# Expert rows scattered into a slot-sorted DRAM table and turned in 32x32 blocks on VectorE, instead of gathered per tile and turned on TensorE

## The chip, the cores and the metric

The kernel runs on one core of a Trainium2 chip. The metric is the device time of one execution in microseconds (us). All five engines (TensorE, VectorE, ScalarE, GpSimd, SyncE) run their own instruction streams, which are written out by hand and meet at semaphores.

## The reference

A gated cross-attention block over 4 batches of 512 tokens with 512 features, then a mixture-of-experts FFN with 16 experts, of which each token takes 4, and a shared FFN.

```python
x = x + jnp.tanh(g_xattn[0]) * _L0_xattn_ref(_layernorm(x), mask, ctx_2048, ctx_2048, wq, wk, wv, wo)
x = x + jnp.tanh(g_ffn[0]) * _L0_ffn_ref(_layernorm(x), Wg, W1, W2, W3, W1s, W2s, W3s)

def _moe_forward(hidden_states, Wg, W1, W2, W3, W1s, W2s, W3s):
    x = hidden_states.reshape(-1, D)                                  # T = 2048 tokens, D = 512
    shared = jax.nn.silu(x @ W1s.T) * (x @ W3s.T) @ W2s.T             # 704 hidden
    probs = jax.nn.softmax((x @ Wg.T).astype(jnp.float32), axis=-1)   # 16 experts
    topk_w, sel = jax.lax.top_k(probs, TOP_K)                         # 4 of them
    combine = jnp.zeros((T, E), x.dtype).at[jnp.arange(T)[:, None], sel].add(topk_w)
    h = jax.nn.silu(jnp.einsum('td,efd->etf', x, W1)) * jnp.einsum('td,efd->etf', x, W3)   # 352 hidden
    routed = jnp.einsum('etf,edf->td', h * combine.T[:, :, None], W2)
    return shared + routed
```

## The kernel before

Every float32 product is made of three products of a high and a low part (`tripled`, the matmuls of L86). A high part is a rounded copy, a low part the difference of the raw value and the high part.

The program has four stages, one after the other, with a barrier of all engines between two of them.

*Attention* (0 to 436 us) goes batch by batch. SyncE loads the batch's x twice (`x_t` for the sums and `r_t` for the residual, 1 MB each) and the context, and stores x2 (the residual stream, 1 MB) and xn2 (the normalised input of the FFN, 1 MB) to DRAM. The router's probabilities and ranks of the experts are made here.

*Routing* (436 to 552 us): TensorE makes the shared FFN of batches 0 and 1 in the class `Shared`: per batch 6 blocks of hidden columns, then 4 row tiles. Beside it VectorE does the routing, in pieces that `work` assigns to places between the shared FFN's own operations (place 0 to 5 stand behind the blocks of the first batch, 6 to 9 behind its row tiles, and so on). Each of the 2048 x 4 choices gets a slot: slots are sorted by expert, and each expert's slots are filled up to a multiple of 128, a tile. With the drawn inputs there are 72 tiles (the expert of most has 4 or 5). `counts` makes the slot numbers from two small matmuls of the masks, `choose` picks the slot and the weight of each choice, `number` splits slot numbers, and `one_hot` writes 128 masks, with which TensorE makes the list `slot_tokens` (which token stands in each slot) in 64 matmuls at the end of the stage. GpSimd subtracts the first expert's weights (`split_expert`: in pieces of 512 columns here), loads the second expert's high part, and gathers tile 0.

*Experts* (552 to 1051 us) walk over the tiles, four in a loop body, on every engine. GpSimd gathers a tile's 128 rows from `xn_dram` by the slot list into one of four buffers `xg`. For tile t TensorE turns the 128x512 rows in four 128x128 transposes into `c_ps_x`, ScalarE copies the high part to `xT_hi`, VectorE subtracts the low part `xT_lo`. TensorE meanwhile makes the output product of tile t-2 (`c_ps_y`), the transposes of the hidden rows of tile t-1 (`c_ps_h`), and then the 24 products of tile t (`c_ps_u`). ScalarE makes `gate`, VectorE `hf`. GpSimd also loads each further expert's weights, high and raw, in three buffers, and subtracts them (3840 + 512 columns). SyncE stores only 16 tiles of zeros, behind the last tile.

*Combining* (1051 to 1168 us): the shared FFN of batches 2 and 3, and 64 indirect gathers (L1596) of each token's four expert rows.

The padding slots of a tile hold token 0 in the list, and their results are never read.

## Time and profile before

| what | value |
|---|---|
| median of 3 runs (lowest, highest) | 1171.72 us (1171.42, 1180.43) |
| the profiled execution | 1170.14 us, span 1168.5 us |
| mean granted TensorE clock | 0.977 |
| TensorE busy | 1106.2 us (95%) |
| VectorE busy | 490.0 us (42%) |
| ScalarE busy | 279.6 us (24%) |
| GpSimd busy | 477.5 us (41%) |
| moved by DMA | 199.70 MB |

The profile is of one execution. The span runs from its first to its last instruction; the execution's own time is 1.6 us longer. In the rows below a line number is the kernel's line, `PE` is TensorE, `DVE` VectorE, `ACT` ScalarE, `POOL` GpSimd and `SPq` SyncE's DMA issues. What stands in brackets is the engine's idle time ahead of the row and what ended it. Matmul starts are exact, their ends modelled, so the pace of TensorE is read from one start to the next.

### The profile page before, as it was taken

The numbers are of one execution on the slowest core, as the hardware profiler recorded it, in microseconds if no ns is written. First come the engines' busy times: TensorE is split into PE (matmuls) and PEld (weight loads), VectorE is DVE, ScalarE is ACT, GpSimd is POOL, SyncE is SP. The second block draws the span as 40 slices with busy tenths as digits, with TensorE's granted clock in tenths as the row PEclk, the third lists the DMA queues.
The fourth block names the chain that finished last, engine by engine and source line by source line (L and its number), as shares of the span: only waits on it lengthen the run. The fifth ranks groups of instructions, "written<-read, shape, count | busy, mean of one in ns | idle before, by whom it ended". The sixth has DMA issues, their size and how long they took to land. (4 is left out here: it accounts for less than half of the span.)

```text
span 1168.5 us, 18611 instructions
## 1 busy us (share of the span) xinstructions
PE 1106.2 (95%) x5666; PEld 940.0 (80%) x5667; DVE 490.0 (42%) x994; ACT 279.6 (24%) x575; POOL 477.5 (41%) x521
## 2 busy tenths in 40 slices
PE   3999999999999959998989999999999999988997
PEld 3888878878878827686879999999999999977775
DVE  2243463445336255996222222222222222225847
ACT  1231131122113002111223333333333333321210
POOL 4720201201100235101665565556656665617763
PEclk9999999999999968899999999999999999998999
DMA  9411320312220528133864666666666666627785
GB/s 348 193 73 73 122 94 1 141 74 72 108 72 0 225 85 297 36 111 96 325 226 162 216 229 229 238 220 222 236 220 229 229 220 229 215 69 237 226 278 162
DMA packets 54209, 199.70 MB, mean 171 GB/s; under 512 B 7009, under 2 KB 7009, under 8 KB 45985
## 3 DMA queue, kind: packets, MB, share of 16 engines
q0 software_dynamic: 21184, 122.44, 30.1%
q1 hardware_dynamic: 22624, 57.98, 13.9%
q10 hardware_dynamic: 10368, 18.88, 4.3%
q8 instruction: 18, 0.29, 0.1%
q14 instruction: 15, 0.11, 0.0%
HBM read 161.51 MB, written 37.75 MB: 171 GB/s over the span
## 5 line engine op out<-in xcount | busy, mean ns | idle before, releaser
L86 PE MATMUL c_ps_u<-expert_hi,xT_hi 128*128 x576 | 192.7, 335 | 2.0 <-DVE xT_lo L1445 1.9
L86 PE MATMUL c_ps_u<-expert_hi,xT_lo 128*128 x576 | 186.0, 323 | 0.0
L86 PE MATMUL c_ps_u<-expert_lo,xT_hi 128*128 x576 | 185.6, 322 | 0.0
L986 POOL TENSOR_TENSOR expert_lo<-expert_raw,expert_hi (+3 forms) x39 | 158.2, 4079 | 19.9 <-issue 14.0
L73 POOL TENSOR_TENSOR idle<-idle 128x1 f32<-128x1 f32 x91 | 17.5, 192 | 232.0 <-PE c_ps_x L1471 141.3
L86 PEld LDWEIGHTS c_ps_u<-expert_hi,xT_hi 128*128 128x128 f32 x576 | 108.8, 189 | 2.9 <-issue 2.9
L86 PEld LDWEIGHTS c_ps_u<-expert_lo,xT_hi 128*128 128x128 f32 x576 | 109.3, 190 | 0.0
L1459 DVE TENSOR_TENSOR hf<-c_ps_u,gate 128x352 f32<-128x352 f32 x72 | 37.8, 525 | 170.3 <-ACT gate L1434 170.3
L86 PEld LDWEIGHTS c_ps_u<-expert_hi,xT_lo 128*128 128x128 f32 x576 | 108.7, 189 | 0.0
L1449 DVE TENSOR_TENSOR hT_lo<-c_ps_h,hT_hi 128x256 fp32r<-128x256 f32 x72 | 30.6, 425 | 181.4 <-ACT hT_hi L1424 181.4
L86 PE MATMUL c_ps_y<-expert_hi,hT_hi 128*128 (+1 forms) x216 | 91.7, 425 | 2.6 <-DVE hT_lo L1450 2.3
L86 PE MATMUL c_ps_y<-expert_hi,hT_lo 128*128 (+1 forms) x216 | 85.8, 397 | 0.0
L86 PE MATMUL c_ps_y<-expert_lo,hT_hi 128*128 (+1 forms) x216 | 85.6, 396 | 0.0
L1362 POOL DMA_INDIRECT xg<-xn_dram,column x72 | 71.4, 992 | 25.2 <-issue 19.9
L1596 POOL DMA_INDIRECT parts<-y_dram,token_slots x64 | 67.4, 1053 | 24.7 <-issue 19.2
L1434 ACT ACTIVATE gate<-c_ps_u 128x352 f32<-128x352 f32 x72 | 33.4, 464 | 181.4 <-PE c_ps_u L86 181.4
L1417 ACT ACTIVATE y<-c_ps_y 128x512 f32<-128x512 f32 x72 | 43.1, 598 | 113.0 <-PE c_ps_y L86 113.0
L417 DVE TENSOR_TENSOR q_lo<-ps_products,q_hi 128x512 fp32r<-128x512 f32 x32 | 22.1, 692 | 110.5 <-ACT q_hi L349 110.5
L292 POOL TENSOR_TENSOR ln_rstd<-ln_var,minus_half 128x4 f32<-128x4 f32 x8 | 8.2, 1028 | 145.3 <-DVE ln_var L430 145.3
L1623 DVE SCALAR_TENSOR_TENSOR total<-parts,combine_weights,total 128x512 f32<-128x512 f32 x64 | 54.2, 846 | 14.0 <-DMA total<-x_dram 8.3
L1445 DVE TENSOR_TENSOR xT_lo<-c_ps_x,xT_hi 128x512 fp32r<-128x512 f32 x72 | 49.8, 692 | 12.7 <-ACT xT_hi L1411 9.5
L349 ACT ACTIVATE q_hi<-ps_products 128x512 fp32r<-128x512 f32 x32 | 19.2, 598 | 149.4 <-PE ps_products L86 149.4
(268 smaller groups left out, 2454.5 us busy)
## 6 DMA issues: line engine op xcount, KB each, us to landing
expert_hi<-we POOLq DMA_DIRECT2D x16, 1920.0 KB, 7.9
expert_raw<-we POOLq DMA_DIRECT2D x14, 1920.0 KB, 13.0
y_dram<-y ACTq DMA_DIRECT2D x72, 256.0 KB, 2.1
ctxT_hi<-ctxT POOLq DMA_DIRECT2D x4, 1024.0 KB, 7.4
ctxT_raw<-ctxT SPq DMA_DIRECT2D x4, 1024.0 KB, 5.6
ctx_raw<-ctx SPq DMA_DIRECT2D x4, 1024.0 KB, 4.8
r_t<-x SPq DMA_DIRECT2D x4, 1024.0 KB, 5.3
ctx_hi<-ctx POOLq DMA_DIRECT2D x4, 1024.0 KB, 6.9
```

What stands on the lines that cost most here:

```text
L86: last = pe.matmul(out, a[i], b[j], start=(n == 0), stop=(n == 3 * len(pairs) - 1))
L349: act.activation(out, ps_m[:, (m.n - 1) % 2, :], ACT.Copy).then_inc(m_hi, 1)
L417: dve.tensor_tensor(lo, ps_m[:, (m.n - 1) % 2, :], hi, ALU.subtract).then_inc(m_free, 1)
L986: last = eng.tensor_tensor(lo, raw, hi, ALU.subtract)
L1362: pool.indirect_dma_start(xg[v][:], None, mem["xn2"], bass.IndirectOffsetOnAxis(ap=at, axis=0)).then_inc(gathered[v], 16)
L1417: act.activation(y[v][:], ps_y[:, v % 2, :], ACT.Copy).then_inc(y_taken, 1)
L1434: act.activation(gate[u][:], ps_u[:, u, 0, 0:FF], ACT.Silu).then_inc(gate_ready, 1)
L1445: dve.tensor_tensor(x[u][1][:], ps_x[:], x[u][0][:], ALU.subtract).then_inc(x_split, 1)
L1449: dve.tensor_tensor(h[u][1][:, 0:2, :], ps_h[:, 0:2, :], h[u][0][:, 0:2, :], ALU.subtract)
L1459: dve.tensor_tensor(hf[u][:], ps_u[:, u, 1, 0:FF], gate[u][:], ALU.mult).then_inc(h_ready, 1)
L1596: pool.indirect_dma_start(parts[v][:, q, :], None, y_d, bass.IndirectOffsetOnAxis(ap=keep["slots"][:, order[c], q:q + 1], axis=0)).then_in ...
L1623: ins = dve.scalar_tensor_tensor(out=total[k][:], in0=parts[c % 4][:, q, :], scalar=keep["weights"][:, order[c], q:q + 1], in1=total[k][:] ...
```

## The change

The list of tokens by slot is gone. Instead the rows themselves are written to a new DRAM table, `sorted` (10752 rows of 512), at their slots, before the experts begin. Five things go with that.

1. *Fills.* While attention runs, SyncE fills the whole table from x, by six DRAM-to-DRAM copies per batch of 0.92 MB each, 22 MB in all, so that padding slots hold finite numbers. They are issued behind the store of xn2 and ahead of the load of `r_t`; the next batch's `x_t` comes behind that.
2. *Routing.* Twelve more row tiles of xn2 are loaded to SBUF (four are there for the shared FFN). The slot numbers move to earlier places: counting from place 3 to 2, choosing the slots to place 3 (all four at once), the weights to 5. GpSimd, behind the first expert's subtraction, scatters every row tile four times, once per choice: 64 indirect DMAs. It then waits for all of them to land. One-hot masks and list matmuls are gone.
3. *Tile loads.* SyncE waits for the scatters and for the shared FFN's last hidden products, loads the first four tiles, each in four DMAs of 32 partitions, and then loads the second expert's raw weights. In the experts' stage it loads each further tile once its buffer is free, behind its 16 stores of zeros. The four DMAs of a tile lay a row's 512 columns out as four quarters on four groups of 32 partitions.
4. *Turning.* VectorE turns the tile in 32x32 blocks within SBUF into `xT`, one tile ahead of TensorE's products; ScalarE's high part and VectorE's low part read `xT` in SBUF instead of PSUM. The blocks leave the features in another order on the partitions, so the rows of W1 and W3 are laid out in that order ahead of the launch (`sides`).
5. *Weight subtraction.* In the experts' stage it is made in pieces of 512 columns (nine instructions instead of two).

```diff
@@ attention, SyncE
+            def fill(k):
+                for n in range(FILLS):
+                    sp.dma_start(sorted_d[k, n], io["x"][0:SORTED // (B * FILLS)]).then_inc(keep["filled"], 16)
...
                 stores(b - 1)
+                fill(b - 1)
 
                 sp.wait_ge(t_ready, b * 16 + 4)
                 sp.wait_ge(xn2_out, b * 16)
                 sp.dma_start(r_t[:], x_d[b]).then_inc(res_in, 16)
...
+            fill(B - 1)
@@ routing, SyncE
+            for tile, at in rows.items():
+                if tile // IT != 1:
+                    sp.dma_start(at[:], xn2_d[tile]).then_inc(rows_in, 16)
...
-            sp.wait_ge(keep["gathered"][0], 16)
+            sp.wait_ge(moved, NT * TOPK * 16)
+            sp.wait_ge(sh.u_ready, 2 * SC)
+            for t in range(QUAD):
+                load_tile(sp, mem, later, t, t, keep["loaded"][t])
             load_expert(sp, later.w_raw, WE, io, 1, keep["second_raw_in"])
@@ routing, GpSimd, behind split_expert
+            def move(tile):
+
+                for q in range(TOPK):
+                    pool.indirect_dma_start(mem["sorted"], bass.IndirectOffsetOnAxis(
+                        ap=keep["slots"][:, tile, q:q + 1], axis=0), rows[tile][:], None).then_inc(moved, 16)
+
+            pool.wait_ge(slots_ready, 1)
+            pool.wait_ge(keep["filled"], B * FILLS * 16)
...
@@ routing, VectorE
-            work = {0: lambda: (rank(), choices()), 1: rest_of_down, 3: counts,
-                    5: lambda: choose((0, 1)), 6: lambda: choose((2, 3)), 7: lambda: (number(), schedule()),
-                    8: lambda: places(range(BUFFERS)), 9: lambda: (turns(), one_hot(0)),
-                    **{at: (lambda j=j: one_hot(j)) for j, at in enumerate(range(10, 17), 1)}}
+            work = {0: lambda: (rank(), choices()), 1: rest_of_down, 2: counts, 3: slots, 5: weights, 7: schedule,
+                    8: lambda: places(range(BUFFERS)), 9: lambda: (turns(), done())}
@@ tile loads
+def load_tile(sp, mem, later, t, v, sem):
+
+    side = P // SIDE
+    tile = mem["sorted"].rearrange("(t g i) (a c) -> t a i g c", g=side, i=SIDE, a=side)[t]
+    for a in range(side):
+        sp.dma_start(later.xg[v][a * SIDE:(a + 1) * SIDE, :, :], tile[a]).then_inc(sem, 16)
@@ experts, SyncE, behind the zero stores
+            with sp.Fori(1, last + 1) as i:
+                for v in range(QUAD):
+                    sp.wait_ge(x_turned, i * QUAD + v - (QUAD - 1))
+                    load_tile(sp, mem, later, i * QUAD + v, v, loaded[v])
@@ experts, GpSimd
-                pool.wait_ge(gathered[v], (t + (QUAD - v)) * 4)
-                pool.tensor_copy(column[v][:], ...
-                hold(nc, nc.gpsimd, keep)
-                gather(v, column[v][:])
...
-                    split_expert(pool, later, base, w_ready)
+                    if later_than(t, 0):
+                        pool.wait_ge(held, e)
+                    split_expert(pool, later, base, w_ready, D)
@@ experts, ScalarE
-                act.activation(x[u][0][:], ps_x[:], ACT.Copy).then_inc(x_hi, 1)
+                act.activation(x[u][0][:], xt[:], ACT.Copy).then_inc(x_hi, 1)
@@ experts, VectorE
+            def turn(t, v):
+                dve.wait_ge(loaded[v], (t + (QUAD - v)) * 16)
+                wait(dve, x_split, t)
+                dve.transpose(xt[:].rearrange("p k (g i) -> p g k i", i=SIDE),
+                              xg[v][:].rearrange("p g (k j) -> p g k j", j=SIDE)).then_inc(x_turned, 1)
...
-                turn(t, u)
+                turn(t + 1, (v + 1) % QUAD)
                 if later_than(t, 0):
                     turn_h(t - 1, 1 - u)
+                low(t + 1, 1 - u)
                 dve.wait_ge(gate_ready, t + 1)
@@ experts, TensorE
-                for k in range(DC):
-                    last = pe.transpose(ps_x[:, k, :], xg[v][:, k * P:(k + 1) * P], keep["ident"][:])
-                last.then_inc(x_turned, 1)
...
-                turn(t, v)
```

The three places below show the engines' instructions in their order, by names and shapes, and what they wait for. First TensorE in the experts' stage, where the products of one tile end and the output product of an earlier tile begins, before:

```order
L86 MATMUL c_ps_u<-expert_lo,xT_hi_3567 128x352
L86 MATMUL c_ps_u<-expert_hi,xT_lo_3568 128x352
L1471 MATMUL c_ps_x<-ident,xg_71 128x128 [waits c_x_split,gathered2]
L1471 MATMUL c_ps_x<-ident,xg_71 128x128 x3
L86 ISA [waits c_h_split]
L86 MATMUL c_ps_y<-expert_hi,hT_hi_3573 128x512
L86 REGISTER_ALU
```

and after:

```order
L89 MATMUL c_ps_u<-expert_lo,xT_hi_3498 128x352
L89 MATMUL c_ps_u<-expert_hi,xT_lo_3499 128x352
L89 ISA [waits c_h_split]
L89 MATMUL c_ps_y<-expert_hi,hT_hi_3504 128x512
L89 REGISTER_ALU
L89 MATMUL c_ps_y<-expert_lo,hT_hi_3504 128x512
```

The transposes of x and with them the wait for the gathered tile are gone from TensorE; the output product follows the last product directly.

Then GpSimd at the end of the routing stage, from the first expert's subtraction to the end of the stage, before (`b_hot_ready` is VectorE's one-hot masks, `b_index_ready` the list of tokens):

```order
L986 TENSOR_TENSOR expert_lo<-expert_raw,expert_hi 128x512 [waits b_first_raw_in,b_first_hi_in]
L986 TENSOR_TENSOR expert_lo<-expert_raw,expert_hi 128x512 x6
L986 TENSOR_TENSOR expert_lo<-expert_raw,expert_hi 128x256
L986 TENSOR_TENSOR expert_lo<-expert_raw,expert_hi 96x512
L977 DMA expert_hi<-we 128x3840 [waits b_hot_ready,b_t_free]
L978 DMA expert_hi<-we_rest 96x512
L1114 DMA xg_69<-xn_dram,slot_tokens 128x512 [waits b_u_ready,b_index_ready]
L1009 UNCONDITIONAL_BRANCH
```

and after (`first_xs` and `rows` are row tiles of xn2; the left-out rows are the other row tiles' scatters, four each):

```order
L991 TENSOR_TENSOR expert_lo<-expert_raw,expert_hi 128x256
L991 TENSOR_TENSOR expert_lo<-expert_raw,expert_hi 96x512
L1123 DMA sorted_dram<-first_xs_73,token_slots 10752x512 [waits b_xs0_in,filled,b_slots_ready]
L1123 DMA sorted_dram<-first_xs_73,token_slots 10752x512 x3
L1123 DMA sorted_dram<-first_xs_74,token_slots 10752x512 [waits b_xs1_in]
L1123 DMA sorted_dram<-first_xs_74,token_slots 10752x512 x3
...
L1123 DMA sorted_dram<-rows_2456,token_slots 10752x512 x4
L982 DMA expert_hi<-we 128x3840 [waits rows_moved,b_t_free,b_scheduled]
L983 DMA expert_hi<-we_rest 96x512
```

The 64 scatters stand between the subtraction and the second expert's load, which waits for them all (`rows_moved`).

Last SyncE's queue around the barrier between routing and experts, before:

```order
L1073 DMA base_dram<-acc_2405 128x512 [waits b_y_free]
L1073 DMA base_dram<-acc_2406 128x512 [waits b_y_free]
L977 DMA expert_raw<-we 128x3840 [waits gathered0]
L978 DMA expert_raw<-we_rest 96x512
L1009 UNCONDITIONAL_BRANCH
L1348 UNCONDITIONAL_BRANCH [waits barrier_Pool_Activation_PE_DVE_SP_release]
L1325 TENSOR_LOAD last_quad [waits c_zeros_ready]
```

and after:

```order
L1084 DMA base_dram<-acc_2440 128x512 [waits b_y_free]
L1084 DMA base_dram<-acc_2441 128x512 [waits b_y_free]
L1297 DMA xg_68<-sorted_dram 32x4x128 [waits b_u_ready,rows_moved]
L1297 DMA xg_68<-sorted_dram 32x4x128 x3
L1297 DMA xg_69<-sorted_dram 32x4x128 x4
L1297 DMA xg_70<-sorted_dram 32x4x128 x4
L1297 DMA xg_71<-sorted_dram 32x4x128 x4
L982 DMA expert_raw<-we 128x3840
L983 DMA expert_raw<-we_rest 96x512
L1014 UNCONDITIONAL_BRANCH
L1354 UNCONDITIONAL_BRANCH [waits barrier_Pool_Activation_PE_DVE_SP_release]
```

Sixteen tile loads stand ahead of the second expert's raw weights and of the barrier, and wait for the scatters.

## Rows read from the trace of the kernel before

**Rows 1.** Windows view: busy us (x instructions) by engine, clock, DMA

```profile
700.00:800.00 100.00, 100.00 (x599) 93.08 (x599) 27.51 (x60) 32.68 (x75) 56.38 (x67) 1.00 0.58 208
```

**Rows 2.** The page's costliest groups: busy us, mean ns, idle us before them

```profile
L1596 POOL DMA_INDIRECT parts<-y_dram,token_slots x64 | 67.4, 1053 | 24.7 <-issue 19.2
...
L1445 DVE TENSOR_TENSOR xT_lo<-c_ps_x,xT_hi 128x512 fp32r<-128x512 f32 x72 | 49.8, 692 | 12.7 <-ACT xT_hi L1411 9.5
```

**Rows 3.** Timeline of a tile boundary: start us, us, engine, line, operation

```profile
700.93 0.60 PE L1471 MATMUL c_ps_x<-ident,xg 128*128 128x128 f32 x4
...
701.29 0.48 PE L86 MATMUL c_ps_y<-expert_hi,hT_hi 128*128 x1
...
701.60 0.40 PE L86 MATMUL c_ps_y<-expert_lo,hT_hi 128*128 x1
...
701.63 0.52 DVE L1459 TENSOR_TENSOR hf<-c_ps_u,gate 128x352 f32<-128x352 f32 x1 [2.21 <-ACT gate L1434]
...
703.46 0.49 PE L1492 MATMUL c_ps_h<-ident,hf 128*128 128x128 f32 x3
```

**Rows 4.** Timeline of the handover from routing to experts

```profile
549.36 0.39 PE L86 MATMUL b_ps_y<-shared_down_hi,b_h_lo 64*128 64x512 f32 x1
...
551.00 0.43 SPq L977 DMA_DIRECT2D expert_raw<-we  x1
...
553.49 0.60 ACT L1411 ACTIVATE xT_hi<-c_ps_x 128x512 fp32r<-128x512 f32 x1 [21.55 <-PE c_ps_x L1471]
...
555.04 0.66 PE L86 MATMUL c_ps_u<-expert_hi,xT_hi 128*128 x1 [1.59 <-DVE xT_lo L1445]
...
558.14 0.35 PE L86 MATMUL c_ps_u<-expert_lo,xT_hi 128*128 x1
```

**Rows 5.** Timeline of VectorE in attention, and late in it

```profile
158.04 2.47 DVE L499 BATCH_NORM_STATS2 ln_stats<-x_t 128x6 f32<-128x512 f32 x4
...
415.15 7.32 DVE L435 TENSOR_SCALAR x_t<-r_t,ln_mv,ln_rstd 128x512 f32<-128x512 f32 x4 [1.15 <-POOL ln_rstd L292]
```

**Rows 6.** Timeline of GpSimd and VectorE in the routing stage

```profile
460.83 12.15 POOL L986 TENSOR_TENSOR expert_lo<-expert_raw,expert_hi 128x512 fp32r<-128x512 f32 x9 [5.88 <-DMA expert_raw<-we_rest]
...
461.53 1.15 DVE L938 TENSOR_TENSOR b_h_lo<-b_h,b_h_hi 128x512 fp32r<-128x512 f32 x1
...
468.04 0.41 DVE L1235 COPY r_within<-b_ps_y 128x256 f32<-128x256 f32 x1
...
477.28 0.43 DVE L1152 TENSOR_TENSOR r_slot<-r_slot,e_base 128x256 f32<-128x256 f32 x1
...
482.51 0.42 DVE L1160 SCALAR_TENSOR_TENSOR r_one<-ranks,r_slot 128x256 f32<-128x256 f32 x1
482.96 0.42 DVE L1162 TENSOR_REDUCE slot_f<-r_one 128x16 f32<-128x256 f32 x1
```

**Rows 7.** Timeline of GpSimd, the second expert's weights

```profile
565.89 9.72 POOL L986 TENSOR_TENSOR expert_lo<-expert_raw,expert_hi  x2 [2.39 <-issue]
```

**Rows 8.** Timeline of GpSimd in the combining stage

```profile
1055.81 0.95 POOL L1596 DMA_INDIRECT parts<-y_dram,token_slots  x1 [0.30 <-issue]
...
1084.25 1.27 POOL L1596 DMA_INDIRECT parts<-y_dram,token_slots  x1 [0.30 <-issue]
```

**Rows 9.** Timeline of SyncE's queue, four places

```profile
130.56 0.40 SPq L243 DMA_DIRECT2D xn_dram<-r_t  x1
...
141.08 0.40 SPq L248 DMA_DIRECT2D x_t<-x  x1
...
554.07 13.41 SPq L1354 DMA_DIRECT2D y_dram<-zeros  x16
...
1053.93 1.87 SPq L855 DMA_DIRECT2D last_xs<-xn_dram  x4
```

**Rows 10.** The DMA issues: KB each, median us from issue to landing

```profile
r_t<-x SPq DMA_DIRECT2D x4, 1024.0 KB, 5.3
...
parts<-y_dram,token_slots POOLq DMA_INDIRECT x64, 4.5
```

162 lines of the change are left out of this document (70 added, 92 removed).

## The prediction

> **What bounds the kernel now.** I read the busy time by stage first. In a stretch of 100 us inside the expert stage TensorE is busy for all of it, at full granted clock, while VectorE has 28 us of work, GpSimd 56 and the DMA engines a share of 0.58 [rows 1]. So there only fewer or shorter TensorE steps shorten the kernel; 599 matmuls in 100 us, at 40 in a tile, are 6.68 us for one of the 72 tiles [rows 1, 2].
>
> The timeline at a tile boundary gives the price of the four transposes. They start at 700.93, the next product at 701.29: 0.36 us of TensorE's pace. The first product after them takes 0.31 until its successor starts (701.29 to 701.60), where nine products in a row take 2.17 us (701.29 to 703.46), which leaves 0.23 for each of the other eight: another 0.08 that I put down to the change of operands [rows 3]. That is 0.36 to 0.44 a tile.
>
> Then the places where TensorE waits. One matters: the handover from routing to experts. Its last product of routing starts at 549.36 and the first expert product at 555.04; before that come VectorE's last total, SyncE's issue of the next expert's raw weights at 551.00, the transposes, ScalarE's high part (0.60 at 553.49) and VectorE's low part [rows 2, 4]. Today the handover costs under 6 us, because all routing work, the one-hot lists included, fits beside TensorE's shared products.
>
> **The change part by part.** *Transposes.* Their four TensorE steps go from every tile. The first tile's lie in the handover, so 71 are left: 71 x 0.36 = 25.6 to 71 x 0.44 = 31.2 us. I take **-31.2**, since the products then follow each other in one form and the restart goes with the transposes. This needs the new chain to fit in a tile's 6.68 us. VectorE's work is 27.51/15 = 1.84 us a tile now [rows 1], and stays, with a 32x32-block transpose on top. The trace has no such transpose; the nearest row for 512 elements a lane is the low part's 0.69 [rows 2], and the far bound is a VectorE operation beside a GpSimd subtraction, 7.32/4 = 1.83 for 512 elements [rows 5]. Even at 1.83 the sum is 3.7 us of 6.68, and the transpose is made a tile ahead. The low part now reads two SBUF tiles instead of PSUM and one; beside a GpSimd subtraction such an operation took 1.15 where it otherwise takes 0.69 [rows 6]. Also covered. The deadline inside a tile is the transposes of h at 703.46, which need hf; hf starts at 701.63 and takes 0.52, so it is 1.3 us early [rows 3]. Without the x transposes that slack is 0.9; the two new VectorE operations stand ahead of the wait for the gate and finish within the 2.21 us that VectorE idles there [rows 3]. Cost taken: 0.
>
> *Weight subtraction.* One expert's takes 9.72 us in two instructions [rows 7]; in nine pieces the first expert's took 12.15, part of it beside VectorE [rows 6]. GpSimd loses up to 2.4 us per expert and is rid of the per-tile gathers, four or five an expert, each an indirect operation of about the same 1.25 us [rows 8]. It is under 60% busy [rows 1]. Cost 0.
>
> *Tile loads on SyncE.* In a dynamic loop one issue takes 13.41/16 = 0.84 us [rows 9], so four take 3.4 of 6.68 us, three tiles ahead. But tile 4's are queued behind the 16 zero stores, those same 13.4 us, then travel; tiles 0 to 3 last 27 us. It should fit; for the crowded start I add **+1** (bounds 0 and 3).
>
> *Routing.* Here the new cost lies. The 64 scatters stand on GpSimd behind the first expert's subtraction and behind the slot numbers. VectorE's counting takes 9.7 us (468.04 to 477.71, the last operation at 477.28 with 0.43), now one place earlier, behind the low part that ended at 462.68 [rows 6]: 472.4. Two shared-FFN operations (0.69 each), eight choosing operations like the ones at 482.51 and 482.96 (0.42 each, 0.45 apart) and a cast, taken at 0.3, follow: **477.7**. GpSimd has finished its subtraction at 472.98 [rows 6], so the slots release it.
>
> No scatter stands in the trace; the nearest operations are the combining stage's 64 indirect gathers, also 128 rows of 2 KB. Undisturbed they start 1.25 apart (0.95 and 0.30 of issue), beside VectorE work one takes 1.27 and 0.30 [rows 8]; all together (67.4 + 19.2)/64 = 1.35 [rows 2]. I take 1.31: 64 x 1.31 = 84 us (bounds 80 and 100, the latter at 1.57 throughout). The data of one gather land 4.5 us after its issue [rows 10]; so all rows are in the table at 477.7 + 84 + 4.5 = **566**. A price below 1.25 has no row, but a write may be issued otherwise than a read, so a gain isn't excluded.
>
> Then SyncE, which waits for those rows: 16 tile-load issues at 1.87/4 = 0.47 [rows 9] are 7.5 us, two weight issues at 0.43, 0.9 [rows 4], and the barrier, taken at 0.4 (today 1.6 us lie between the end of such issues and ScalarE's high part, the transposes among them): 574.9. All engines stand behind that barrier, since the loads are issued ahead of it. Behind it transpose 0.69, high 0.60, low 0.69 and 0.1: first product at **576.6** instead of 555.04, **+21.5** (with the bounds above 17 to 38). TensorE's 64 one-hot products and VectorE's 128 one-hot operations vanish ahead of this wait and so give nothing: TensorE would just reach the wait earlier. TensorE ran at half clock after the handover, until 558.14 [rows 4]; after a longer gap I expect the same stretch again, no difference.
>
> The Trainium skill speaks against this part (SBUF — State Buffer, "SBUF: two separate sides"): certain VectorE modes lock GpSimd out of a port they share, and GpSimd then cannot write the descriptors of the DMAs that it issues. The 0.95 that becomes 1.27 beside VectorE agrees in direction; by the page the cadence follows VectorE's mix of work, and that is the slower rival below.
>
> *Fills.* Per attention batch six DRAM-to-DRAM copies of 0.92 MB go on SyncE's queue ahead of r_t and x_t. A 1 MB load lands in 5.3 us [rows 10]; 5.5 MB read and written are 14 us if a copy moves like a load, 28 if both ways count. x_t's load was issued at 141.08 and first needed at 158.04, 17 us later, without idle time ahead of it [rows 5, 9]; so it can be held some 11 us. The copies start with the issue behind xn2's store at 130.56 [rows 9]: at 14 us they are through by 145, 4 us into that reserve, at 28 by 159, some 6 beyond it. Cost taken **0**, being nearest to the load's row, bounds 0 and 10 (5 us in two batches).
>
> **Sum.** Against the profiled execution's 1170.1: -31.2 + 21.5 + 1 + 0 = -8.7, that is 1161.4. The median shown is 1.6 above that execution, so **1163**. A measurement of this kernel can hardly tell less than 1% from nothing; the forecast is 0.75% faster, so "same" is its class, but the edge at 1160.0 is only 3 us away.
>
> **The rivals.** *(a) Scatters are cheap.* At a cadence under 1.07 us all rows are in place by 551.0, when SyncE's queue is free of routing [rows 4]; then only the tile loads' issue, the barrier and the first tile's parts are left, 10.6 us: first product near 561.6 or a little earlier, +6.5, and with -31.2 and +1 the time is 1171.7 - 23.7 = 1148. Against it: every indirect operation in this trace has over 0.94 of execution. 0.08.
>
> *(b) Scatters are slow, and the kernel with them.* Scatters run while VectorE computes shared products, choices and schedule; if each waits on average half of a 0.7 us VectorE operation, the cadence is 1.31 + 0.35 = 1.66 and the first product 22 us later still: 1163 + 22 = 1185. Slower than 1183.4 it decides from a cadence of 1.63. For it: 1.27 against 0.95, and the other way round 1.83 for a VectorE operation of 512 elements beside GpSimd, against 2.47/4 = 0.62 [rows 5, 8]. Against: VectorE loses 128 operations in the very stretch, and is half idle. 0.14.
>
> *(c) Fills delay attention.* The queue's order makes r_t and x_t wait for copies; VectorE then is late for the next batch's sums and TensorE idles some 5 us in two batches: 1163 + 10 = 1173. 0.13.
>
> *(d) The gain is not collected.* If the block transpose takes over 3 us, or the tiles come late, VectorE's chain binds at a boundary, and the removed 0.44 comes back as a wait: 1163 + 15 to 31, 1178 to 1194. For it: no row shows the operation or loads in 512-byte runs. Against: 2.2 us of idle and a tile of lead. 0.10. The Trainium skill gives 311 ns for a 128x128 bf16 transpose on VectorE (VectorE: DVE Perf Modes, "The three transpose paths"); no run here shows one, and by that figure four blocks' worth would be some 1.2 us, as an estimate, which is covered as well.
>
> **How the numbers follow.** The forecast as described has 0.55, with 1155 to 1175 as its own range; with (a) to (d) that is 1. Faster than 1160.0: 0.26 of the forecast and all of (a), 0.34. Slower than 1183.4: most of (b), a third of (d), a little of (c), 0.17. Same: 0.49. The range for 8 in 10 reaches from 1150, leaving out most of (a), to 1186, leaving out the upper part of (b) and (d).
>
> **What would show it.** In the profile after: no TensorE transposes of x, a tile in about 6.24 us; 64 indirect stores on GpSimd from about 478 to 562 with 1.25 to 1.35 between starts; TensorE idle from about 547 to 576 with SyncE's tile loads last in the chain; VectorE's block transpose below 2 us; no idle time of TensorE in attention that ends on x_t or r_t. Wrong it would be above all by the scatters' cadence, since it counts 64 times: 0.1 us is 6.4 us.

## The result, and the profile after

The changed kernel took **1203.35 us** (median of 4 executions, 1201.46 to 1205.81) against 1173.01 for the kernel before on the same chip (4 executions, 1171.42 to 1180.43): ratio 1.0247, 95% interval 1.0199 to 1.0296, so 2.5% slower. Forecast were 1163 and a range of 1150 to 1186. The profiled execution took 1203.38 us, its span is 1201.8 at a mean granted clock of 0.949 (0.977 before).

I cut each span at the same two places: the first expert product, and the first transpose of the combining stage (`d_ps_t`).

| us | before | changed | difference | changed, `again` (below) | difference |
|---|---|---|---|---|---|
| start to the first expert product | 555.0 | 622.7 | +67.6 | 582.3 | +27.3 |
| from there to the first `d_ps_t` | 496.2 | 459.1 | -37.0 | 458.9 | -37.2 |
| from there to the end | 117.3 | 120.0 | +2.7 | 119.2 | +1.9 |
| span | 1168.5 | 1201.8 | +33.3 | 1160.4 | -8.1 |

The expert stage gave what was forecast and more (-37.0 against -31.2 and +1). The windows of the changed kernel, in the columns of [rows 1], first beside the scatters and then inside the expert stage:

```profile
504.00:558.00 54.00, 14.73 (x30) 7.31 (x28) 1.62 (x7) 0.00 (x0) 41.03 (x43) 0.55 0.57 217
...
740.00:840.00 100.00, 100.00 (x578) 93.02 (x577) 42.53 (x80) 34.07 (x80) 49.89 (x48) 1.00 0.69 234
```

In the lower row TensorE is busy throughout, now with 578 matmuls where there were 599 [rows 1]; at 36 instead of 40 in a tile that is 6.23 us a tile against 6.68. The upper row is the surprise: in 54 us of the routing stage TensorE ran 30 matmuls. The page's groups (mean ns in the second column behind the bar) and its DMA issues show the new operations:

```profile
L1596 POOL DMA_INDIRECT parts<-y_dram,token_slots x64 | 67.4, 1054 | 26.6 <-issue 19.0
...
L1451 DVE TENSOR_TENSOR xT_lo<-xT,xT_hi 128x512 fp32r<-128x512 f32 x73 | 61.4, 842 | 1.4 <-ACT xT_hi L1410 1.4
L1446 DVE STREAM_TRANSPOSE xT<-xg 128x512 f32<-128x512 f32 x73 | 51.4, 704 | 11.5 <-PEq L1014 9.4
...
sorted_dram<-x SPq DMA_DIRECT2D x24, 896.0 KB, 13.2
xg<-sorted_dram SPq DMA_DIRECT2D x292, 64.0 KB, 2.9
```

The block transpose takes 0.70 us, close to the 0.69 used as its nearest row. The low part went from 692 to 842 ns on average and hides, as said.

The timeline of the routing stage and the handover, by engine:

```profile
479.57 0.20 DVE L1189 CAST token_slots<-slot_f 128x64 int32<-128x64 f32 x1
...
480.06 1.10 POOL L1123 DMA_INDIRECT sorted_dram<-first_xs,token_slots  x1 [8.94 <-DVE token_slots L1189]
...
535.16 0.59 PE L89 MATMUL b_ps_u<-b_xT_hi,shared_up_hi 128*128 128x512 f32 x1 [2.21 <-issue]
537.97 0.59 PE L89 MATMUL b_ps_u<-b_xT_lo,shared_up_hi 128*128 128x512 f32 x1 [2.21 <-issue]
540.77 0.59 PE L89 MATMUL b_ps_u<-b_xT_hi,shared_up_lo 128*128 128x512 f32 x1 [2.21 <-issue]
...
561.55 0.97 POOL L1123 DMA_INDIRECT sorted_dram<-rows,token_slots  x1 [0.30 <-issue]
564.90 0.59 POOL L982 DMA_DIRECT2D expert_hi<-we  x1 [2.38 <-DMA sorted_dram<-rows,token_slots]
...
570.19 1.08 ACT L923 ACTIVATE b_silu<-b_ps_u 128x512 f32<-128x512 f32 x2 [78.80 <-remote]
...
611.41 7.51 SPq L1297 DMA_DIRECT2D xg<-sorted_dram  x16
618.97 0.43 SPq L982 DMA_DIRECT2D expert_raw<-we  x1
...
620.27 0.53 POOL L1371 MEMSET zeros<- 128x512 f32 x1 [54.23 <-POOLq L1014]
620.33 0.71 DVE L1446 STREAM_TRANSPOSE xT<-xg 128x512 f32<-128x512 f32 x1 [9.38 <-PEq L1014]
...
622.66 0.66 PE L89 MATMUL c_ps_u<-expert_hi,xT_hi 128*128 x1 [12.57 <-DVE xT_lo L1451]
```

The scatters nearly keep the forecast: first at 480.06, last at 561.55, 1.29 us apart, all landed by 564.9. But the tile loads start only at 611.41, because SyncE also waits for the shared FFN's last hidden products, and its totals stand ahead of the loads; both come from TensorE, and TensorE had *crawled*. From 505.7 on gaps open between its matmuls of `b_ps_u`; from 515.5 to 557.6 they start 2.1 to 2.8 us apart (2.80 each from 532 on), where the same ones are otherwise 0.23 apart. What ended the idle time is "issue", and these matmuls carry no wait of their own: TensorE waited for no engine and no data that the profile shows. It also reported late. ScalarE's `b_silu` at 570.19 uses products whose matmul ended at 508.2; the record of that semaphore's rise is 62 us later. The waits of TensorE in this stretch (us in total, times, longest):

```profile
PE b_ps_u L89 <- issue: 39.3, 23, 2.2
PE b_ps_u L89 <- DVE b_h L954: 13.4, 1, 13.4
PE c_ps_u L89 <- DVE xT_lo L1451: 12.6, 1, 12.6
```

The last shared product starts at 609.7; in `again`, a run of the same program that keeps its pace, at 549.8. Matmul by matmul, most of these 60 us come up to the end of the crawl: 39 of idle time on "issue" and some 8 because each matmul takes 0.59 us in place of 0.23. Of the rest, 13.4 are the wait for a late report. Below, "the crawl" means this pair: TensorE's instructions spread out, and its semaphore updates late.

### The profile page after: what moved, and what is told of

Its sections match the earlier page's. It is cut to its first block and busy times, and to the rows that moved or that the text cites. A ratio compares the mean times of both kernels' runs of the same rounds, so it can differ in the third digit from the quotient of the medians.

```text
span 1201.8 us, 18739 instructions
## 1 busy us (share of the span) xinstructions
PE 1077.4 (90%) x5314; PEld 909.7 (76%) x5315; DVE 514.3 (43%) x935; ACT 276.2 (23%) x576; POOL 466.4 (39%) x468
## 5 line engine op out<-in xcount | busy, mean ns | idle before, releaser
L991 POOL TENSOR_TENSOR expert_lo<-expert_raw,expert_hi (+1 forms) x144 | 184.1, 1313 | 218.1 <-DMA expert_raw<-we_rest 207.8
L89 PE MATMUL c_ps_y<-expert_hi,hT_hi 128*128 (+1 forms) x216 | 85.6, 396 | 2.3 <-DVE hT_lo L1456 2.3
L89 PE MATMUL b_ps_u<-b_xT_hi,shared_up_hi 128*128 128x512 f32 x88 | 39.0, 443 | 32.0 <-DVE b_h L954 19.3
L1451 DVE TENSOR_TENSOR xT_lo<-xT,xT_hi 128x512 fp32r<-128x512 f32 x73 | 61.4, 842 | 1.4 <-ACT xT_hi L1410 1.4
L1446 DVE STREAM_TRANSPOSE xT<-xg 128x512 f32<-128x512 f32 x73 | 51.4, 704 | 11.5 <-PEq L1014 9.4
L89 PE MATMUL b_ps_u<-b_xT_hi,shared_up_lo 128*128 128x512 f32 x88 | 37.8, 429 | 16.4 <-issue 16.4
## 6 DMA issues: line engine op xcount, KB each, us to landing
sorted_dram<-x SPq DMA_DIRECT2D x24, 896.0 KB, 13.2
```

The source lines that it names most:

```text
L89: last = pe.matmul(out, a[i], b[j], start=(n == 0), stop=(n == 3 * len(pairs) - 1))
L991: last = eng.tensor_tensor(lo, raw, hi, ALU.subtract)
L1446: dve.transpose(xt[:].rearrange("p k (g i) -> p g k i", i=SIDE), xg[v][:].rearrange("p g (k j) -> p g k j", j=SIDE)).then_inc(x_turned, 1)
L1451: dve.tensor_tensor(x[u][1][:], xt[:], x[u][0][:], ALU.subtract).then_inc(x_split, 1)
```

## The experiments

Each kernel was compared with the kernel before on its own chip. The runs from `late_scatter` to `choice_order` ran on two chips (15 and 8), and none of them showed the crawl; that this was not the kernels' doing only became plain with `again`. A run without an interval is a single execution.

**late_scatter** puts the scatters behind the whole shared FFN of the stage:

```diff
             pool.wait_ge(keep["filled"], B * FILLS * 16)
+            pool.wait_ge(sh.y_free, 2 * IT)
```

> The changed kernel, but GpSimd starts the 64 scatters only when VectorE has taken all eight output products of the shared FFN. Theory 1 (TensorE crawls because indirect DMAs stream beside it): without them beside it TensorE's last shared product stands near 547 us again, as in the kernel before, where the changed kernel had 609.7; the scatters then run alone for 64 x 1.28 = 82 us, and the first expert product comes near 547 + 82 + 3 + 12 = 644 to 648 instead of 622.7: about 1225 us. Rival (the routing stage is slow for another reason, as the other order of VectorE's pieces or the twelve row loads): the last shared product stays near 600, and the total goes to 1280 or so.

Measured 1227.6 us beside 1172.8. The last shared product started at 545.3, the first expert product came at 646.0, and no semaphore of TensorE was late:

```profile
646.02 0.66 PE L89 MATMUL c_ps_u<-expert_hi,xT_hi 128*128 x1 [100.33 <-DVE xT_lo L1452]
```

So moving the scatters behind the products costs 100 us of waiting. It does not show that their being side by side caused the crawl, since this chip (15) did not crawl with them side by side either.

**read_instead** reads with 64 indirect gathers by the same slot numbers instead of writing with 64 scatters (the table holds filler alone). It also waits ahead of every sixth gather, so that at most twelve are under way, which the scatters do not:

```diff
-                    pool.indirect_dma_start(mem["sorted"], bass.IndirectOffsetOnAxis(
-                        ap=keep["slots"][:, tile, q:q + 1], axis=0), rows[tile][:], None).then_inc(moved, 16)
+                pool.indirect_dma_start(own[n % len(own)][:], None, mem["sorted"], bass.IndirectOffsetOnAxis(
+                    ap=keep["slots"][:, n // TOPK, n % TOPK:n % TOPK + 1], axis=0)).then_inc((moved, moved2)[group], 16)
```

> The changed kernel with 64 indirect gathers of the same size (out of the filled table, by the same slot numbers, into the row buffers) in place of the 64 scatters, so the table holds only filler and the experts work on that. Theory A (it is the writing into DRAM that holds TensorE up): TensorE's last shared product near 547, the last gather lands near 564, first expert product near 577, total 1155 to 1160 us. Theory B (a stream of indirect DMAs in either direction does it): shared products crawl as in the changed kernel, total 1195 to 1205.

1164.3 beside 1172.8, last shared product at 547.5, first expert product at 581.3. That is the unaltered kernel's time on this chip (below): where there is no crawl, the direction of the transfer costs nothing.

**fills_only** is the kernel before with the 24 fills and the table, and nothing else:

```diff
                 stores(b - 1)
+                fill(b - 1)
```

> The kernel before with only the 24 copies that fill the table, and the table's 22 MB in DRAM ahead of the later tables; nothing reads it. If the copies cost nothing in attention (the changed kernel's trace has VectorE's and TensorE's waits there as before): 1170 to 1174 us. Rival C (it is the place of the tables in DRAM that makes indirect DMAs disturb TensorE): the combining stage shows updates of TensorE's semaphores some 5 to 15 us late, as in the changed kernel, and takes 120 us instead of 117; under theories A and B it shows none.

1172.67 beside 1172.76, one execution each: the fills cost nothing that shows, rival (c) is out.

**bounce** keeps the list and the gathers per tile, stores each tile to DRAM and loads it back in quarters, and turns it on VectorE; there is no scatter:

```diff
+            def store(t, v):
+                sp.wait_ge(gathered[v], (t + (QUAD - v)) * 4)
+                sp.dma_start(table[t], xg[v][:]).then_inc(stored[v], 16)
...
+                for v in range(QUAD):
+                    store(i * QUAD + v, v)
+                    load(i * QUAD + (v - 1), (v - 1) % QUAD)
```

> The kernel before with its list of tokens and its gathers per tile; each gathered tile is stored to DRAM by SyncE and loaded back in column quarters, then turned in blocks on VectorE as in the changed kernel; the zero stores stand at the end of SyncE's queue; weights subtracted in 512-column pieces. No scatters, no fills. If the block transposes are worth what the changed kernel's expert stage shows (457 instead of 494 us from first to last product, of which 71 x 0.44 = 31 by the tile), and the first tile's way through DRAM costs about 8 us: 1170 - 31 to 37 + 8 = 1141 to 1147 us. Rival (the extra 512 KB of DMA per tile, or SyncE's five issues of 0.84 us, bind): a tile takes 6.7 us or more, total above 1170.

1283.1, a clear miss of mine. The pace is 6.25 us a tile, but TensorE waits once per expert (waits view, expert stage):

```profile
PE c_ps_y L87 <- DVE hT_lo L1490: 101.5, 16, 9.8
PE c_ps_u L87 <- DVE xT_lo L1485: 18.1, 1, 18.1
```

The releaser named is the end of a chain: VectorE is in order, and its turn of the next tile stands ahead of `hT_lo`. That tile is late, since GpSimd's gather waits behind an expert's weight subtraction and its loads; gathering further ahead is the test of that.

**bounce_far** is `bounce` with the gathers 12 tiles ahead and the stores 8:

```diff
+AHEAD = 3 * QUAD
...
-            for v in range(1, QUAD):
-                gather(v, keep["index"][:, v:v + 1])
+            for n in range(1, AHEAD):
```

> The bounce kernel with gathers 12 tiles ahead instead of 4, and stores to the table 8 ahead. In the bounce kernel a tile took 6.25 us, but TensorE waited 101 us in 16 waits of up to 9.8 us for tiles, about one per expert, when GpSimd was held up by an expert's weights. If that is all: first product near 567, 72 tiles at 6.25 with the rest as in the changed kernel (457 us), combining 117 to 120: 1142 to 1150 us. If the extra traffic or SyncE binds: above 1170.

1209.1 beside 1173.8, a miss again: the 16 waits shrink to 41.1 us, and tile 4 comes 18 us late, since SyncE's load of it stands behind a store that waits 21.0 us for a gather. This fits the reading of `bounce`, and the scatters' merit is now visible: the table takes GpSimd out of the per-tile chain, and its 27 us at the handover are cheaper than these stalls.

**half_scatter** issues two of the four scatters per row tile, so half of the table keeps filler:

```diff
-                for q in range(TOPK):
+                for q in range(TOPK // 2):
```

> The changed kernel with 32 of the 64 scatters (two of the four choices of each row; the other slots hold filler, so those experts' rows are of other values). Theory 1 (each scatter that runs beside TensorE holds it up, while they run): TensorE crawls from about 504 to 521, when the scatters end, and then goes on as in the kernel before: last shared product 547 + 17 = 565 to 570, first expert product 575 to 582, total 1155 to 1163 us. Theory 2 (something fills up over the first 16 or so scatters and has to drain by itself): the semaphore updates of TensorE come late for long after the last scatter, first expert product above 590, total above 1170.

1141.75 beside 1173.8. The handover is nearly gone:

```profile
561.52 0.66 PE L89 MATMUL c_ps_u<-expert_hi,xT_hi 128*128 x1 [12.58 <-DVE xT_lo L1451]
```

Rival (a) priced a table that is ready early at a first product near 561.6, and 1148; the place was right to 0.1 us. With the rows there in time, the rest of the change is worth 32 us on this chip (single executions), or 28 by the spans of the traces (1140.1 against 1168.5).

**paired_scatter** allows two scatters under way, on two semaphores:

```diff
+                    own = (moved, moved2)[n % 2]
+                    if n > 1:
+                        pool.wait_ge(own, n // 2 * 16)
```

> The changed kernel with at most two scatters under way: each waits until the one two before it has landed. If it is a backlog of writes that holds TensorE up, it is gone: the scatters take 64 x 1.3 to 1.9 us, and TensorE's last shared product stands near 547; first expert product 15 us behind the last landing, 580 to 615, total 1158 to 1195. If one or two writes at a time suffice to hold TensorE up, the last shared product stays beyond 600 and the total at 1203 or more.

1185.8: a cadence of 1.66, last scatter at 585.6, first product at 604.4, the shared FFN undisturbed. This is the price rival (b) gave, 1185, for a cadence of 1.66.

**linear_stores** replaces each scatter by a plain store of the same size from GpSimd (the table's rows then stand in another order), with two idle operations ahead of it to keep the pace:

```diff
+                    pool.dma_start(table[tile * TOPK + q], rows[tile][:]).then_inc(moved, 16)
```

> The changed kernel with 64 plain stores of the same size, from the same row tiles, issued by GpSimd at about the same pace, each to 128 rows that follow each other, in place of the scatters (so the table holds rows in another order). Theory A1 (any stream of writes to DRAM at 200 GB/s does it): TensorE crawls as in the changed kernel, total 1190 to 1205. Theory A2 (it takes indirect writes): last shared product near 547, total near 1160.

1171.9: last store at 569.5, first product at 587.7, no crawl. The stores are 1.35 us apart, but that is the idle operations' doing: the plain store itself occupies GpSimd for 0.56 us, a scatter for 0.97. So the run says nothing of what a table filled by plain stores would cost.

**again** is the changed kernel, unaltered, on chip 15:

> The changed kernel, unaltered. In its first runs TensorE crawled beside the scatters (first expert product at 622.7) and took 1201 to 1206 us, but kernels with 32 scatters, with scatters in pairs, with plain stores and with gathers in their place ran undisturbed. If the crawl belongs to the kernel, it comes again: 1201 to 1206 us, ratio 1.02 to 1.03. If it was a condition of the chip or of those executions, the last scatter lands at 564.5, the first expert product stands near 577, 6.25 us for a tile, and combining takes 117: 1203.4 - 45.7 - 2.7 = 1155 us, ratio 0.985.

**1164.7 us** (1162.03 to 1165.9) against 1174.05, ratio 0.9928 (0.9902 to 0.9954): the same program is 0.7% faster here. Its windows and its handover:

```profile
500.00:560.00 60.00, 50.23 (x213) 38.90 (x212) 15.10 (x35) 7.03 (x12) 45.68 (x48) 0.96 0.67 249
```

```profile
504.79 0.39 PE L89 MATMUL b_ps_u<-b_xT_hi,shared_up_lo 128*128 128x512 f32 x1
505.02 0.39 PE L89 MATMUL b_ps_u<-b_xT_hi,shared_up_hi 128*128 128x512 f32 x1
...
549.27 0.50 PE L89 MATMUL b_ps_y<-shared_down_hi,b_h_hi 64*128 64x512 f32 x1
...
563.60 0.97 POOL L1123 DMA_INDIRECT sorted_dram<-rows,token_slots  x1 [0.30 <-issue]
566.34 8.23 SPq L1297 DMA_DIRECT2D xg<-sorted_dram  x16
567.53 0.56 POOL L983 DMA_DIRECT2D expert_hi<-we_rest  x1
...
574.60 0.50 SPq L982 DMA_DIRECT2D expert_raw<-we  x1
575.15 0.49 SPq L983 DMA_DIRECT2D expert_raw<-we_rest  x1
579.92 0.52 POOL L1371 MEMSET zeros<- 128x512 f32 x1 [11.83 <-POOLq L1014]
579.97 0.71 DVE L1446 STREAM_TRANSPOSE xT<-xg 128x512 f32<-128x512 f32 x1 [28.88 <-PEq L1014]
...
582.30 0.66 PE L89 MATMUL c_ps_u<-expert_hi,xT_hi 128*128 x1 [32.07 <-DVE xT_lo L1451]
```

Beside the same scatters TensorE runs at 0.23 us a matmul, its last shared product starts at 549.8, and the handover is the forecast one, 5.7 us later (582.3 against 576.6). All rows are in the table at 566.3, as forecast, but the barrier does not open when SyncE is through at 575.6. It opens at 579.9: GpSimd issued its last load at 567.53 and passed the barrier 11.83 us after it was done with that. In between GpSimd runs one instruction, the barrier's own drain (567.40 to 579.67), and it outlasts the load: the load has landed at 576.76, and the barrier opens 3.16 us later. In all ten traces where this load is the last thing that GpSimd does and GpSimd comes last, the distance from landing to barrier is 3.15 or 3.16 us. In the first run SyncE came last, and the barrier opened 0.4 us after its last issue (619.87, 620.27).

**slim_handover** leaves tiles 1 to 3 and the zero stores behind the barrier, to shorten SyncE's part:

```diff
-            for t in range(QUAD):
-                load_tile(sp, mem, later, t, t, keep["loaded"][t])
+            load_tile(sp, mem, later, 0, 0, keep["loaded"][0])
```

> The changed kernel with only the first tile's four loads ahead of the barrier, the other twelve behind it, and the zero stores at the end of SyncE's queue. 12 x 0.47 = 5.6 us less between the last landing and the first product. Without the crawl: 1155 - 5.6 = 1149 to 1150. With it (first product set by the last shared product near 610): 1203 - 5.6 = 1198.

1161.9, ratio 0.9908 (0.9879 to 0.9937): 2.8 us less than `again` where 5.6 were forecast, and the executions of the two overlap. The first product at 580.7 is no gain of the handover. This execution's scatters began 1.7 us earlier (479.84 against 481.55), and from the first scatter to the first product it takes 100.9 us, `again` 100.8. With SyncE's 12 issues out of the way the barrier still opened only at 578.35, so GpSimd sets it. What the edit did gain is the late tile 5 (1.1 us, below), since the zero stores no longer stand ahead of its loads.

**choice_order** scatters choice by choice instead of tile by tile:

> The changed kernel with the same 64 scatters in another order: the first choice of all 16 row tiles, then the second, and so on. Same number, same pace. If the crawl comes with 64 unbroken scatters beside TensorE, it comes here too: 1195 to 1206. If it hangs on the execution or on the order, the time is as in the undisturbed case, near 1155.

1164.5: no difference, on a chip that doesn't crawl with either order.

**hi_behind** is `slim_handover` with GpSimd's load of the second expert's high part moved behind the barrier, so that GpSimd has nothing under way there:

```diff
-            load_expert(pool, later.w_hi, WE, io, 1, keep["w_in"])
...
+            load_expert(pool, later.w_hi, WE, io, 1, w_in)
```

> The slim kernel with GpSimd's load of the second expert's high weights issued behind the barrier instead of ahead of it. In the repeated runs of the changed kernel GpSimd reached the barrier only 12 us after this load's issue (579.9, where SyncE was ready at 575.6), and in the slim kernel it alone set the barrier at 578.4. If that drain is the cause, the barrier now stands 3.5 us after the last landing, the first expert product 6 us after it instead of 16: 10 us less than the repeated changed kernel and 1.3 us less for the fifth tile's wait, about 1153 us. If the barrier waits for something else, the time stays at 1161 to 1162.

1213.2 beside 1182.3, ratio 1.0248 (1.0207 to 1.0289). This was on chip 13, and the crawl was back, last shared product at 610.9. The kernel before was slow there too: 1182.3 against 1172.8 to 1174.5 on every other chip; it wasn't profiled there.

**again_2** ran the unaltered changed kernel beside it, on chip 13:

> The changed kernel once more. TensorE crawled beside the scatters in its first four executions (1201 to 1206 us) and in none of the four later ones (1162 to 1166). If the crawl hangs on the chip or its condition, this run shows one of these two and nothing between: 1162 to 1166 without, 1201 to 1206 with; a value between would say that its size varies from execution to execution.

1209.1, ratio 1.0231 (1.0173 to 1.029), with the first run's picture (waits of TensorE, and ScalarE's timeline):

```profile
PE b_ps_u L89 <- issue: 44.2, 25, 2.2
```

```profile
567.80 1.09 ACT L923 ACTIVATE b_silu<-b_ps_u 128x512 f32<-128x512 f32 x2 [78.95 <-remote]
```

So one program is 0.7% faster on one chip and 2.3% slower on another, and nearly all of the difference lies in one stretch of one stage.

**hi_behind_2** repeats `hi_behind`; it fell on chip 3, without the crawl:

> The kernel with the second expert's high weights loaded behind the barrier, once more, since its first executions had the crawl (last shared product 611.3). Where TensorE does not crawl: barrier 3.5 us after the last landing, first expert product near 572, about 1153 us (ratio to the kernel before 0.983). Where it crawls: 1207 to 1217 again.

1164.6, ratio 0.9911 (0.988 to 0.994), some 10 us more than I expected. The handover did shrink, and the gain went in tile 1:

```profile
566.03 1.77 SPq L1295 DMA_DIRECT2D xg<-sorted_dram  x4
...
572.67 0.59 POOL L982 DMA_DIRECT2D expert_hi<-we  x1 [8.41 <-POOLq L1014]
...
574.54 0.66 PE L89 MATMUL c_ps_u<-expert_hi,xT_hi 128*128 x1 [24.62 <-DVE xT_lo L1452]
...
584.86 0.71 DVE L1447 STREAM_TRANSPOSE xT<-xg 128x512 f32<-128x512 f32 x1 [10.55 <-DMA xg<-sorted_dram]
```

The barrier opened at 572.2 instead of 578.35, though the last scatter landed 1.5 us later than in `slim_handover` (566.01 against 564.53): 6.2 us behind it instead of 13.8. So GpSimd's load was what held it. But tile 1's four loads were issued only from 572.16 and their rows could be turned only at 584.86, beside the two weight loads.

**read_2** and **pair_2** are `read_instead` and `paired_scatter` once more, on the same chip 3:

> 64 indirect gathers in place of the 64 scatters. Where the scatters make TensorE crawl: if writing does it, last shared product near 548 and 1164 to 1170; if any unbroken stream of indirect DMAs does it (as the late semaphore updates in the combining stage of the crawling executions, beside gathers, suggest), TensorE crawls here too and the kernel takes 1200 or more. Where there is no crawl: 1164 as before.

> At most two scatters under way. Where the unaltered scatters make TensorE crawl (to be read from hi_behind_2 beside it): if the crawl is a backlog, this kernel has TensorE's last shared product near 548 there too and takes 1186; if one or two writes at a time suffice, its last shared product lies beyond 600. Where there is no crawl: 1186 as before.

1169.2 and 1183.5. Meant to be tried on a crawling chip, they fell on one that doesn't crawl, and tell nothing new of its cause.

**two_ahead** is `hi_behind` with tiles 0 and 1 loaded ahead of the barrier, which is open to SyncE anyway until GpSimd comes:

```diff
-            load_tile(sp, mem, later, 0, 0, keep["loaded"][0])
+            for t in range(2):
+                load_tile(sp, mem, later, t, t, keep["loaded"][t])
```

> The changed kernel with both halves of the handover mended: SyncE loads expert tiles 0 and 1 (8 loads) before the barrier and the other two behind it, GpSimd's load of the second expert's high parts stands behind the barrier, and the zero stores are issued at the end. In hi_behind_2 the barrier let go at 572.2 and the first expert product began at 574.5, but tile 1's rows, whose loads stood behind the barrier, came only at 584.9, and TensorE waited 8.1 us for it, and the two tiles after it lost 1.5 more. If that late load is all that ate the gain: first product at 574 to 575 again, no wait in tile 1, expert and combining stages as before it, so 1162.5 - 8.1 - 1.5 = 1153 to 1156 us, where TensorE is not slowed beside the scatters. Rival: the early barrier only lets eight loads and the second expert's weights collide, and the wait moves to tile 2 or 3: 1160 to 1165. On a chip like the one of again_2, TensorE crawls beside the 64 scatters and the time is near 1210 whatever the handover does, since the last shared product then ends near 610.

**1159.4 us** (1151.62 to 1162.13, 5 executions) against 1174.5, ratio 0.9864 (0.9847 to 0.988), on chip 6, without the crawl; the profiled execution took 1151.6. Its first product:

```profile
570.06 0.66 PE L89 MATMUL c_ps_u<-expert_hi,xT_hi 128*128 x1 [25.91 <-DVE xT_lo L1453]
```

The wait for rows is all but gone. VectorE still waits for tile 2's, and TensorE loses 1.4 us behind it:

```profile
581.78 0.71 DVE L1448 STREAM_TRANSPOSE xT<-xg 128x512 f32<-128x512 f32 x1 [4.47 <-DMA xg<-sorted_dram]
```

The profiled execution lies just under the forecast 1153 to 1156, but part of that is luck: its first scatter stands at 476.53, 5.0 us earlier than in `again` and `hi_behind_2`, and no edit did that. From the first scatter to the first product it takes 93.5 us, where `hi_behind_2` took 93.0 and `again` 100.8. The median lies 3 above the forecast; the executions spread over 10 us, and what differs between them wasn't profiled.

**pair_3** ran beside it:

> The changed kernel with at most two scatters under way, a third time, beside two_ahead, which keeps the unbroken stream of 64. If two_ahead shows the crawl in this call (last shared product near 610), this run tells for the first time whether waiting for each scatter's predecessor but one ends it on such a chip: last shared product near 547 and 1184 if it does, near 610 and above 1210 if the number of scatters or their target is the cause whatever their spacing. If two_ahead shows no crawl, this run can only repeat 1184 to 1186 and tells nothing new of the cause.

1185.8. `two_ahead` showed that this chip doesn't crawl, so this only repeats the price.

## Why the prediction was wrong

**The step that failed** is in the part on routing: "TensorE's 64 one-hot products and VectorE's 128 one-hot operations vanish ahead of this wait and so give nothing: TensorE would just reach the wait earlier." It takes for granted that the shared FFN keeps its pace beside the 64 scatters. In the first run it didn't: the last shared product came near 610 instead of 547, SyncE's loads followed at 611, and the term +21.5 measured +67.6. The range covered slow scatters, not a slow TensorE; no row of before has indirect writes beside products in such a stream. Rival (b), slower, had the right side of before and the wrong mechanism: the cadence was 1.29, below even the 1.31 taken, and all rows were in the table by 564.9 (forecast 566).

**Term by term,** where TensorE kept its pace (`again`):

- *Transposes*, -31.2 forecast. From one tile's `c_ps_h` to the next, before lies 38.9 us above 6.25 a tile over the 71 steps. 7.8 of these are two boundaries that are longer than 6.68 (13.86 and 7.33 us), the other 31.1 are the forecast term. The sum over the stage was -37.2, and the excess is in the main a stall that I had passed over in the trace of before:

```profile
591.90 0.78 PE L1471 MATMUL c_ps_x<-ident,xg 128*128 128x128 f32 x4 [4.63 <-DMA xg<-xn_dram,column]
```

  TensorE waits 4.63 us there, and the matmuls behind it start 0.43 us apart instead of 0.23, at a granted clock of 0.79. Tile 4's gather was late behind the second expert's subtraction and loads; the change loads that tile on SyncE, and the stall went with it. This was to be found before: it is TensorE's longest wait in the stage (the next is 2.3 us, in the last tile).
- *Weight subtraction* in pieces, 0: no wait of TensorE in the changed kernel ends on it. *Zero stores*, +1: in `again` the step from tile 4 to 5 takes 7.38, 1.1 over the pace. *Fills*, 0: `fills_only` confirms it, but the working was off. At [rows 10]'s 5.3 us for 1 MB, six copies of 0.92 MB are 29 us one after another, not 14; measured, a batch's six take 21.7 us from the first issue to the last landing (131.0 to 152.7), and still nothing waits.
- *Handover*, +21.5: measured +27.3 in `again`. Of the missing 5.8 some 3.9 are the barrier, taken at 0.4 and measured at 4.3 behind SyncE's last issue, because it opens only when GpSimd's last load has landed; `hi_behind_2` opened it earlier by moving that load. Another 0.9 are SyncE's issues, at 0.51 us a load instead of 0.47. 0.3 is a slip of the sum, whose own parts (574.9, then 0.69, 0.60, 0.69 and 0.1) make 577.0 and not 576.6. That the rows were in by 566.3, where 566 was forecast, is two errors in one: the first scatter came at 481.6 instead of 477.7, and the last one landed 2.7 us after its issue instead of 4.5, at a slightly shorter cadence.
- *Combining*, taken as unchanged: +1.9. Its largest wait is 3.5 us for `d_h_lo`; the cause is open.
- Sum: +27.3 - 37.2 + 1.9 = -8.0, against -8.7 forecast. Three errors cancel: +5.8 in the handover, -7.0 in the expert stage (-37.2 against -30.2, the stall above all) and +1.9 in combining. The 1164.7 of `again` owes its closeness to the forecast 1163 to that luck.

**The rivals.** (a) was wrong in its condition and right in its place and near in its price (`half_scatter`). (c) and (d) are out: routing's first product came at 433.3 us, where three kernels without fills have it at 433.4 to 436.0, and the transpose is at 0.70 us.

**The port rule.** The prediction cited the Trainium skill (SBUF — State Buffer, "SBUF: two separate sides") for scatters slowed by VectorE. The trace agrees in direction, and the effect is small. In `again` six of the 64 scatters took 1.10 to 1.71 us instead of 0.97, and each of the six stands beside a VectorE operation with two input tiles (`b_h_lo`, the schedule's `grid`); 28 others beside VectorE work did not grow. Together that is 1.9 us over the 64, and the cadence was 1.30, 1.29 in the first run. So the direction was right, and the price of the rival built on it, 0.35 us a scatter, was some ten times too high.

**What stays open** is the cause of the crawl. It appears in the first run's trace and in both traces on chip 13 (`again_2`, `hi_behind`), and in none on chips 15, 3 and 6 with the same stream of 64 scatters. Each chip but 15 was visited once, so the chip and the hour can't be told apart. In those three traces it is not confined to the scatters. The combining stage, where GpSimd *reads* with 64 indirect gathers beside TensorE's products, shows it on a smaller scale (waits of the first run, from 1080 to the end):

```profile
PE d_ps_u L89 <- issue: 3.3, 3, 1.7
PE d_ps_y L89 <- issue: 2.3, 1, 2.3
```

That is 5.6 us there, 5.9 in `again_2` and 5.2 in `hi_behind`, with semaphores of TensorE up to 23 us late; in every other trace it is 0. So indirect writes are not needed for it.

The three traces share one more thing: updates of the semaphore that counts the landings are missing from the record. 64 scatters make 1024 updates. The traces without the crawl that have all 64 show 1022 to 1024 of them, the first run 164, `again_2` 154 and `hi_behind` 143. Beside the 64 gathers it is 1028 against 373, 417 and 369. GpSimd still saw them all, since it went on at 564.9. So semaphore updates, or the records of them, pile up or get lost where TensorE crawls. Whether the pile-up holds TensorE, whether TensorE's own late updates are part of it, and whether recording itself brings it about, no run here shows: every time in this document comes from a recorded execution.

Excluded is data: the crawling matmuls carry no wait. Instruction fetch is unlikely: the fetches near this stretch (at 477.6, 522.2 and 596.5) took about 1 us each, as in `again`. By the Trainium skill (Runtime: NRT & Kernel Launch, "Instruction fetch mechanics") they come in blocks of 16 KB and are mostly hidden; the trace agrees on the size, with 18 such packets of 16 KB in the whole execution. The clock is not the start of it: the first gaps stand at 505.7, and the granted clock fell to the lower of its two levels, 1.2 GHz, at 509.7. At that level the same matmuls are otherwise 0.43 us apart (476.0 to 478.6), not 2.80. The kernels that would tell whether it is the writes, their number or their spacing say nothing: `read_instead`, `read_2`, `pair_2` and `pair_3` ran on chips that don't crawl with all 64 either, and chip 8, where `half_scatter`, `linear_stores` and `paired_scatter` ran, never had the unbroken stream of 64; its traces show no crawl beside the combining stage's gathers, so it probably doesn't crawl either.

## What to carry to other kernels

When a change puts a long stream of GpSimd's DMAs beside TensorE's work, look at the pace of TensorE in that stretch on more than one chip before you believe a gain of under 3%: here the same program stood at 0.993 and at 1.025. GpSimd held the barrier until the DMA that it had issued last had landed, so an early load there can cost more than it hides; and once the barrier opens earlier, the next tile's loads must have been issued too. Read the stage that you leave alone for its largest single wait; it may be removed by the change without your having meant it. And before you credit an edit with a microsecond or two, measure from a common event (here the first scatter): executions of one program came to that event 4 us apart (481.55 in `again`, 477.42 in `again_2`).

## What the hardware showed unexpectedly

- TensorE issuing one `b_ps_u` matmul per 2.1 to 2.8 us for 42 us without waiting for anything in the profile, and a semaphore of its rising 62 us after the matmul that carries it, while 860 of 1024 updates of the scatters' semaphore are missing from the record; in three traces (first run, `again_2`, `hi_behind`), beside indirect writes and, less, beside indirect reads, and in none on chips 15, 3, 6 and 8.
- GpSimd's drain at a barrier outlasts its last DMA: the barrier opened 3.16 us after the landing of a 1.9 MB load, 12.4 us after its issue (`again`). With no such load it opened 6.2 us after the last scatter's landing (`hi_behind_2`, `two_ahead`).
- Indirect writes of 128 rows of 2 KB cost GpSimd what indirect reads do: 0.97 + 0.30 us, against 0.95 + 0.30 [rows 8].
- A transpose of 128x512 float32 values in 32x32 blocks on VectorE, 0.70 us.
- DRAM-to-DRAM copies of 0.9 MB, six issued in a row: the first lands 7.3 to 7.6 us after its issue, the others 2.4 to 3.6 us after one another (median from issue to landing 13.2).
